# Three fp32r passes for the expert down product, with the first weights split once and streamed from DRAM

## Chip, cores and metric

One core of one Trainium2 chip. The metric is device time of one execution in microseconds. The kernel before has a median of 554.55 us over 3 runs (554.51 to 554.79).

## What is computed

The reference is a stack of four layers over `x` (128 sequences of 32 steps, 128 features). Each layer has a conditioning block and a feed-forward block. The change touches the feed-forward block of layer 0 only. It is a mixture of 8 experts in which each expert chooses `cap = 8` steps of each sequence:

```python
scores = jnp.einsum('BTC,CE->BTE', x, gate_w)
probs = jax.nn.softmax(scores, axis=-1)
top_p, top_idx = jax.lax.top_k(jnp.transpose(probs, (0, 2, 1)), cap)
xin = jnp.take_along_axis(x[:, None, :, :], top_idx[..., None], axis=2)
h = jax.nn.gelu(jnp.einsum('BElC,ECH->BElH', xin, w1), approximate=False)   # C=128, H=512
y = jnp.einsum('BElH,EHC->BElC', h, w2) * top_p[..., None]
out = jnp.zeros((B, T, C), x.dtype).at[b_idx, top_idx].add(y)
```

Before it stands the layer's own mixture of 2 shared and 8 routed experts, which every step passes through. Behind it stand an LSTM, a quantised convolution block, a tanh RNN, a ternary block, a leaky RNN and a gated block, which the change leaves alone apart from three waits at their start.

## The kernel before

Everything is kept transposed (features on the 128 partitions). Every engine's program is written out by hand; semaphores tie them together, and nothing is reordered later. Four stretches matter here.

**Chunk stage.** The steps are cut into 8 chunks of 512 columns. Chunks 0 and 1 are a special start. Each of chunks 2 to 7 (`chunk`) has 12 units, of which every third is a shared one and the rest are routed. For a routed unit TensorE (PE) makes the first product, ScalarE (ACT) the gelu (`routed_gelu`, L452), VectorE (DVE) the multiplication with the gate (`routed_gated`, L456), ACT the high half of the hidden values (`hidden_high`, L372), GpSimd (POOL) the low half (`hidden_low`, L387: values minus high half), and PE the second product. A product of split operands is `product`: three fp32r matmuls (L325 high·high, L326 high·low, L327 low·high). First products run 3 units ahead of second ones. In the unit with index 3, ACT also makes the high half of the next chunk's x, and POOL the low half behind unit 6 (L318).

**Expert stage.** 4 groups of 8 tiles, 8 experts in each, and 2 halves (b = 0, 1) of each expert's 512 hidden rows: 64 steps w. `expert_up(w)` is `product` twice over 256 columns into a PSUM bank; ACT's gelu (L1442) writes SBUF (`hb`, the old `th` and `pb` tiles); `expert_down(w)` is 2 plain fp32 matmuls with `w2` (L1248, two records each in the trace); DVE copies the result out (`output_copy`, L1382). PE issues `expert_up(w + 3)` and then `expert_down(w)`. The first weights of each expert are split anew in each group on DVE (`expert_split`, L1219 high, L1221 low; 32 times) into the two tile pairs `sw1_hl` and `sw3_hl`.

**Beside the experts.** In group g the tokens of group g+1 are gathered: one-hot tables on DVE (L1160), token halves (L1172 ACT, L1180 DVE), gather products on PE (L1198) behind steps 5, 7, 9 and 11, copies out on ACT (L1210). The results of group g are turned (L1299, behind step 14 and behind the next group's first step), copied by ACT (L1308), and scattered (L1316) with tables from DVE (L1371). Group 0 also makes the second half of the choice of steps (softmax with a table load on ACT at L1058, top 8 on DVE at L1081 and L1082, rows to DRAM at L1096) and the mean absolute weights (L219) that POOL's preparation of later weights needs.

**SP's queue.** SyncE (SP) issues all DMAs in order: expert weights with two 256 KB loads a chunk (`load_expert`), the gates' rows, the gather rows (L1155), raw weights (L206), slot rows (L1103), convolution taps (L211).

Of the kernel before, what the change touches and what calls it, by code (L numbers as in the profile page):

```python
# [15 lines left out]
P = 128  # L16
# [3 lines left out]
E = 8  # L20
# [33 lines left out]
def build_program(nc, t, out):  # L54
# [8 lines left out]
    with ctx:  # L63
# [32 lines left out]
        with ExitStack() as layer0:  # L96
# [4 lines left out]
            gate_w = sb0("gate_w", [P, E])  # L101
            w1 = sb0("w1", [P, E, H0])
            w2 = sb0("w2", [P, E, HT, C])

# [16 lines left out]
            i_dram = nc.dram_tensor("topi_scratch", [NTILE, SLOT_TILE], F32, kind="Internal").ap()  # L121

# [3 lines left out]
            s_wmoe, s_gw, s_wffn, s_sw2 = [sem(f"s_wmoe{k}") for k in range(5)], sem("s_gw"), sem("s_wffn"), sem("s_sw2")  # L126
# [87 lines left out]
            def weight_sums():  # L214

                dve.wait_ge(s_w1, n_late)
                dve.wait_ge(s_raw, 48)
                for k, w in enumerate(raw_weights()):
                    dve.tensor_reduce(wsum[:, k:k + 1], w, X, ALU.add, apply_absolute_value=True).then_inc(s_sum, 1)  # L219
# [47 lines left out]
            cst = in_x1("cst", 1024, CHUNK)  # L267
            th = [sb0(f"th{k}", [P, CHUNK]) for k in range(2)]
            pb = [sb0(f"pb{k}", [P, CHUNK]) for k in range(2)]
# [21 lines left out]
            ctok_low0 = sb0("ctok_low0", [P, CHUNK], F32R)  # L291
            stage_b = layer0.enter_context(ExitStack())
# [171 lines left out]
            def chunk(c, par, last=False):  # L464
# [29 lines left out]
                for u, (kind, j) in enumerate(units):  # L494
# [31 lines left out]
                for u, (kind, j) in enumerate(units):  # L526
# [31 lines left out]
                    if c == CHOICE_CHUNK + 1 and u == 4:  # L558
                        choice_rows(0)
                if last:  # L560
                    for q in range(2):
                        gather_copy(q, (1,), dve, s_gxl)
                    dve.wait_ge(s_wffn, 32 * E)
                    expert_split(0)
                    for q in range(2, 4):
                        gather_copy(q, (1,), dve, s_gxl)
                    expert_split(1)
                if not last:
                    load_gate_rows(c + 1, 1 - par)
                if c == 2:  # L570
# [10 lines left out]
                load_expert(c)  # L581

            def load_expert(c):
                sp.dma_start(w1[:, ds(c, 1), :], t["f_w1"][:, ds(c, 1), :]).then_inc(s_wffn, 16)
# [2229 lines left out]
```

## Time and profile before

| what | value |
|---|---|
| runs | 554.51, 554.55, 554.79 us |
| span of the profiled execution, first to last instruction | 553.3 us |
| what lies around it, from the runs' median | 1.25 us |
| PE busy | 540.1 us, 98% |
| DVE, ACT, POOL busy | 425.7, 380.6, 197.8 us |
| chain that ended last | PE 81%, DVE 12%, ACT 4%, issue 2%, POOL 1% |
| granted PE clock | full in all 40 slices |

The page gives the span of the profiled execution; its own time is not shown apart from that. A matmul's recorded duration includes the part that overlaps the next one, so the cost of a matmul in a stream is read from start to start, or from the chain, and not from its mean duration. The same holds for ACT and DVE: an instruction that waits for nothing starts about 0.1 us before the one ahead of it has ended.

### The profile page before, as it was taken

The page shows a single profiled execution, that of the slowest core. Times are in us where ns is not written, and L with a number is a line of the kernel's source. Part 1 is how long each engine was busy: PE and PEld are TensorE (multiplying, and loading weights), DVE is VectorE, ACT ScalarE, POOL GpSimd, SP SyncE. Part 2 cuts the span into 40 slices and gives each one's busy share as a digit, 9 for nine tenths or more (in the row PEclk, how much of TensorE's full clock was granted, in tenths as well). Part 3 has the DMA queues.
Part 4 walks back from the last instruction along what each step waited for, and adds up shares of the span by engine and source line. Part 5 has one row for each costly group of instructions (what it writes and reads, how often), then busy time and mean ns, then how long its engine had stood idle before and what let it go on. Part 6 is the DMA issues. An engine that isn't in the chain of part 4 may idle for free.

```text
span 553.3 us, 10078 instructions
## 1 busy us (share of the span) xinstructions
PE 540.1 (98%) x3341; PEld 468.0 (85%) x3341; DVE 425.7 (77%) x1026; ACT 380.6 (69%) x857; POOL 197.8 (36%) x186
## 2 busy tenths in 40 slices
PE   8999999999999999999999989999999999999997
PEld 7877888887887899999999877788989999987785
DVE  4987656567659779676856359998999999999866
ACT  4567767758767664454552246888988888888965
POOL 4688788788788402947100000010000000000100
PEclk9999999999999999999999999999999999999999
DMA  8634306512081302021000000122111111112211
GB/s 285 194 152 159 152 1 230 191 56 97 2 305 43 124 10 82 1 73 62 2 1 1 0 1 2 20 39 21 21 20 20 21 31 30 34 38 47 45 52 39
DMA packets 30227, 37.36 MB, mean 68 GB/s; under 512 B 20096, under 2 KB 23648, under 8 KB 29280
## 3 DMA queue, kind: packets, MB, share of 16 engines
q1 hardware_dynamic: 30176, 36.72, 21.2%
q8 instruction: 28, 0.46, 0.4%
q14 instruction: 23, 0.19, 0.1%
HBM read 30.24 MB, written 2.28 MB: 59 GB/s over the span
## 4 chain that ended last, share of the span: by engine, by line
PE 81%; DVE 12%; ACT 4%; issue 2%; POOL 1%; DVEq 0%; ACTq 0%
PE bank L325 11%; PE bank L1248 10%; PE bank L327 10%; PE bank L326 10%; PE bank L1673 4%; PE bank L1759 4%; PE bank L1663 4%; PE bank L1700 3%; PE bank L1701 3%; PE bank L1316 2%; PE bank L1198 1%; PE bank L1748 1%; PE bank L1786 1%; PE bank L409 1%; PE bank L1772 1%
## 5 line engine op out<-in xcount | busy, mean ns | idle before, releaser
L387 POOL TENSOR_TENSOR hidden_low<-hidden,hidden_high 128x512 fp32r<-128x512 f32 x72 | 94.4, 1318 | 24.6 <-ACT hidden_high L372 22.4
L2054 POOL CAST h_high<-h 128x256 fp32r<-128x256 f32 x15 | 6.4, 426 | 197.6 <-ACT h L1865 191.2
L452 ACT ACTIVATE bank<-bank 128x512 f32<-128x512 f32 x56 | 32.6, 583 | 34.5 <-PE bank L327 34.3
L456 DVE TENSOR_TENSOR hidden<-bank,big 128x512 f32<-128x512 f32 x56 | 38.5, 688 | 15.8 <-ACT bank L452 14.6
L372 ACT CAST hidden_high<-hidden 128x512 fp32r<-128x512 f32 x70 | 43.0, 615 | 3.3 <-DVE hidden L456 1.9
L1700 PE MATMUL bank<-taps_high,q1T 128*128 128x512 f32 x94 | 42.9, 457 | 1.0 <-ACT q1T L1828 0.6
L325 PE MATMUL bank<-xin_high,sw_high 128*128 128x256 f32 x128 | 43.9, 343 | 0.0
L1701 PE MATMUL bank<-taps_low,q1T 128*128 128x512 f32 x94 | 37.1, 395 | 0.0
L1382 DVE COPY yT<-bank 128x256 f32<-128x256 f32 x32 | 13.6, 424 | 30.4 <-PE bank L1248 30.4
L1801 ACT ACTIVATE gates_t<-bank,lstm_b_half 128x128 f32<-128x128 f32 x96 | 28.2, 364 | 12.2 <-PE bank L1673 8.8
L1663 PE MATMUL bank<-x,lstm_wx 128*128 128x128 f32 x256 | 34.4, 277 | 1.7 <-ACT gates_t L1801 0.9
L326 PE MATMUL bank<-xin_low,sw_high 128*128 128x256 f32 x128 | 36.1, 282 | 0.0
L327 PE MATMUL bank<-xin_high,sw_low 128*128 128x256 f32 x128 | 35.9, 280 | 0.0
L1663 PEld LDWEIGHTS bank<-x,lstm_wx 128*128 128x128 f32 x256 | 32.0, 191 | 4.4 <-ACT gates_t L1801 3.3
L1442 ACT ACTIVATE pb<-bank 128x512 f32<-128x512 f32 x32 | 19.5, 608 | 22.7 <-PE bank L327 22.7
L1673 PE MATMUL bank<-hL,lstm_wh 128*128 128x128 f32 x256 | 34.1, 276 | 0.5 <-DVE hL L1927 0.4
L1673 PEld LDWEIGHTS bank<-hL,lstm_wh 128*128 128x128 f32 x256 | 32.3, 192 | 2.4 <-DVE hL L1927 1.4
L998 POOL TENSOR_TENSOR hidden_low<-hidden,hidden_high 128x512 fp32r<-128x512 f32 x24 | 30.8, 1287 | 9.4 <-ACT hidden_high L778 9.0
L1248 PE MATMUL bank<-pb,w 128*128 128x256 f32 x128 | 32.8, 378 | 0.0
L1248 PE MATMUL bank<-th,w 128*128 128x256 f32 x128 | 32.7, 378 | 0.0
L1759 PE MATMUL bank<-g,ffn_w 128*128 128x256 f32 (+1 forms) x136 | 30.7, 368 | 0.0
L1874 ACT ACTIVATE g<-bank,ffn_b 128x256 f32<-128x256 f32 (+1 forms) x68 | 27.6, 467 | 1.0 <-PE bank L1749 0.6
(270 smaller groups left out, 1736.6 us busy)
## 6 DMA issues: line engine op xcount, KB each, us to landing
big<-gates_scratch SPq DMA_DIRECT2D x7, 2048.0 KB, 8.1
w<-in_f_w SPq DMA_DIRECT2D x16, 256.0 KB, 6.2
onehot<-topi_scratch SPq DMA_DIRECT2D x8, 512.0 KB, 4.2
outT<-x SPq DMA_DIRECT2D x15, 128.0 KB, 2.1
xT<-in_xT SPq DMA_DIRECT2D x3, 512.0 KB, 7.4
hidden<-in_ffn_w SPq DMA_DIRECT2D x3, 256.0 KB, 5.2
hidden<-in_conv_w SPq DMA_DIRECT2D x3, 256.0 KB, 4.8
xT<-in_xT SPq DMA_DIRECT2D x2, 256.0 KB, 4.2
```

The costliest lines, as they stand in the source:

```text
L325: pe.matmul(dst, wh[:, cols], vh[:, :], start=start, stop=False)
L326: pe.matmul(dst, wh[:, cols], vl[:, :], start=False, stop=False)
L327: return pe.matmul(dst, wl[:, cols], vh[:, :], start=False, stop=stop)
L372: act.copy(hidden_hl[u % 3][0][:, :], hidden[u % 3][:, :]).then_inc(s_hi, 1)
L387: pool.tensor_tensor(hidden_hl[u % 3][1][:, :], hidden[u % 3][:, :], hidden_hl[u % 3][0][:, :].bitcast(F32), ALU.subtract).then_inc(s_lo, 1)
L456: dve.tensor_tensor(hidden[u % 3][:, :].rearrange("p (i k) -> p i k", k=P), r_bank[j % 2][:, :].rearrange("p (i k) -> p i k", k=P), gate_r ...
L1248: mm = pe.matmul(y_bank[e % 2][:, 0:SLOT_GE], w2[:, e, ht, :], hb[w % 4][:, i * SLOT_GE:(i + 1) * SLOT_GE], start=(ht == 0), stop=(ht == H ...
L1663: mm = pe.matmul(gate_ps(t, q), lstm_wx[:, q * P:(q + 1) * P], x1[:, t, :], start=(0 < t < EARLY or (t > 0 and q == 0)), stop=(t == 0), sk ...
L1673: mm = pe.matmul(gate_ps(t, q), lstm_wh[:, q * P:(q + 1) * P], hL[:, (t - 1) % 2, :], start=(t == 0), stop=(t > 0), skip_group_check=True)
L1700: pe.matmul(dst, q, taps_high[:, 2 - j, :], start=True, stop=False)
L1701: pe.matmul(dst, q, taps_low[:, 2 - j, :], start=False, stop=True).then_inc(c_taps, 1)
L1759: mm = pe.matmul(bank_down(v), ffn2_w2[:, f, :], part(g2[:, f, :, :], v), start=(f == 0), stop=(f == HT - 1))
```

## The change

The down product becomes `product` with `w2` and the gelu's result both split: 6 fp32r matmuls a step in place of 2 fp32 ones. `w2` is split once, in place. The gelu (`expert_gelu`) now writes back into its PSUM bank, ACT makes the high half of it (`expert_high`), DVE the low half (`expert_low`), in 3 buffer pairs in place of 4 buffers. `w1` is split once in the chunk stage (ACT high, DVE low, at the units in `PARTS_AT`, and `w2` 3 units behind each), its halves are stored to DRAM and loaded for each expert of each group (32 times, 512 KB) into one of 3 tile pairs. `expert_split` goes. Core of the diff:

```diff
+            w2_high = nc.alloc_sbuf_tensor_at("w2_high", [P, E, H0], F32R, offset=at_w1)
+            w2_low = nc.alloc_sbuf_tensor_at("w2_low", [P, E, H0], F32R, offset=at_w2)
+            w1_dram = nc.dram_tensor("w1_parts_scratch", [E, 2, P, H0], F32, kind="Internal").ap()
...
@@ chunk, ACT
+                    if n * c + u in PARTS_AT:
+                        w1_high_part(PARTS_AT.index(n * c + u))
+                    if n * c + u - 3 in PARTS_AT:
+                        w2_high_part(PARTS_AT.index(n * c + u - 3))
@@ chunk, DVE
+                    if n * c + u - 1 in PARTS_AT:
+                        w1_low_part(PARTS_AT.index(n * c + u - 1))
+                    if n * c + u - 4 in PARTS_AT:
+                        w2_low_part(PARTS_AT.index(n * c + u - 4))
                 if last:
-                    for q in range(2):
+                    for q in range(4):
                         gather_copy(q, (1,), dve, s_gxl)
-                    dve.wait_ge(s_wffn, 32 * E)
-                    expert_split(0)
...
+                for e in STORE_PARTS[c]:
+                    store_parts(e)
...
+            PARTS_AT = (28, 35, 42, 49, 55, 73, 79, 85)
+            STORE_PARTS = {2: (0,), 3: (1, 2), 4: (3, 4), 5: (5,), 6: (), 7: (7,)}
...
+            def w1_low_part(e):
+                dve.wait_ge(s_w1hi, e + 1)
+                dve.tensor_tensor(w1_third[1][:, :], w1[:, e, :], w1_third[0][:, :].bitcast(F32), ALU.subtract
+                                  ).then_inc(s_w1lo, 1)
...
+            def load_parts(k):
+                if k == 0:
+                    sp.wait_ge(s_ab, 2 * NSH * NCHUNK)
+                    sp.wait_ge(s_w1st, 32 * E)
+                if k >= 3:
+                    sp.wait_ge(s_h, 2 * (k - 2))
+                for part_no, dst in enumerate(w1_hl[k % 3]):
+                    sp.dma_start(dst[:, :].bitcast(F32), w1_dram[k % E, part_no]).then_inc(s_w1ld[k % 3], 16)
...
@@ expert_up
-                    pe.wait_ge(s_es, 2 * (g * E + e + 1))
+                    pe.wait_ge(s_w1ld[k % 3], 32 * (k // 3 + 1))
...
-                    pe.wait_ge(s_hg, w - 3)
+                    pe.wait_ge(s_hbl, w - 3)
@@ expert_down
-                pe.wait_ge(s_hg, w + 1)
+                pe.wait_ge(s_hbl, w + 1)
...
-                    mm = pe.matmul(y_bank[e % 2][:, 0:SLOT_GE], w2[:, e, ht, :], hb[w % 4][:, i * SLOT_GE:(i + 1) * SLOT_GE],
-                                   start=(ht == 0), stop=(ht == HT - 1))
+                    h_parts = [hl[w % 3][:, i * SLOT_GE:(i + 1) * SLOT_GE] for hl in (hb_high, hb_low)]
+                    mm = product(y_bank[e % 2][:, 0:SLOT_GE], (w2_high[:, e, :], w2_low[:, e, :]),
+                                 slice(ht * P, (ht + 1) * P), h_parts, ht == 0, ht == HT - 1)
...
+            def expert_gelu(w):
+                act.wait_ge(s_h, w + 1)
+                act.activation(h_bank[w % 4][:, :], h_bank[w % 4][:, :], ACT.Gelu).then_inc(s_hg, 1)
+
+            def expert_high(w):
+                act.wait_ge(s_hg, w + 1)
...
+                if w >= 3:
+                    act.wait_ge(s_y2, w - 2)
+                act.copy(hb_high[w % 3][:, :], h_bank[w % 4][:, :]).then_inc(s_hbh, 1)
+
+            def expert_low(w):
+                dve.wait_ge(s_hbh, w + 1)
...
+                dve.tensor_tensor(hb_low[w % 3][:, :], h_bank[w % 4][:, :], hb_high[w % 3][:, :].bitcast(F32), ALU.subtract
+                                  ).then_inc(s_hbl, 1)
...
@@ group_sp
+                for e in range(E):
+                    k = g * E + e + 3
+                    if k < GROUPS * E:
+                        load_parts(k)
+                    if g == 0 and e == 3:
+                        choice_store(1)
+                    if g == 0 and e == 4:
+                        sp.wait_ge(s_vc, 64)
+                        load_slots(1)
```

DVE's order in a group is rewritten around `expert_low`; the four weight sums (`weight_sum`) are spread over two experts; the tap loads move from behind group 2 into groups 1 and 2.

**ACT at the start of the expert stage** (`th`, `pb`, `bank` and `hb` are the gelu's targets, `sel` is the softmax's). Before:

```order
L417 COPY cst<-bank 128x512
L1210 CAST xin_high<-bank 128x8x64
L1442 ACTIVATE th<-bank 128x512 x2
L1058 ACT_TABLE_LOAD
L1058 ACTIVATE sel<-score 128x128
L1442 ACT_TABLE_LOAD
L1442 ACTIVATE pb<-bank 128x512
```

and with the change:

```order
L1315 ACTIVATE bank<-bank 128x512
L1323 CAST hb_high<-bank 128x512
L1315 ACTIVATE bank<-bank 128x512
L1323 CAST hb_high<-bank 128x512
L1121 ACT_TABLE_LOAD
L1121 ACTIVATE sel<-score 128x128
L1315 ACT_TABLE_LOAD
L1315 ACTIVATE bank<-bank 128x512
L1323 CAST hb_third<-bank 128x512
```

Two casts now stand ahead of the two table loads, and one more between them and the third step's down product.

**DVE in group 0, around the second half of the choice.** With the change (L1329 is `expert_low`, L1461 the output copy, L1144 and L1145 the top 8, L1153 the last of the rows, L1226 a one-hot table, L1450 scatter tables):

```order
L1461 COPY yT<-bank 128x8x32
L1329 TENSOR_TENSOR hb_low<-bank,hb_high 128x512
L1246 TENSOR_TENSOR ctok_low<-ctok,ctok_high 128x512
L1144 MAX topv<-probT 128x8
L1145 MAX_INDEX topi<-topv,probT 128x8
L1144 MAX topv<-probT 128x8
L1145 MAX_INDEX topi<-topv,probT 128x8
L1152 CAST topf<-topi 128x32
L1153 TENSOR_TENSOR topf<-topf,seq_off 128x32
L1226 TENSOR_SCALAR onehot<-onehot,part 128x1024
L1450 TENSOR_SCALAR scat<-iota_tok,slot_cols 128x128 x2
L1329 TENSOR_TENSOR hb_low<-bank,hb_high 128x512
```

A low half on which a down product waits now stands behind all of these, where a weight split stood.

**SP in group 0.** With the change (L646 loads the two halves of one expert's weights, L1159 stores the rows of the choice, L1166 loads the slot rows):

```order
L646 DMA w_third_high<-w_parts_scratch 128x512
L646 DMA w_third_low<-w_parts_scratch 128x512
L646 DMA sw_high<-w_parts_scratch 128x512
L646 DMA sw_low<-w_parts_scratch 128x512
L1159 DMA topi_scratch<-topf 128x32
L1159 DMA topv_scratch<-topv 128x32
L646 DMA sw_high<-w_parts_scratch 128x512
L646 DMA sw_low<-w_parts_scratch 128x512
L1166 DMA slot_rows<-topi_scratch 32x128
```

The load for the group's last expert stands behind the store of the rows.

## Rows read from the trace of the kernel before

**Rows 1.** The page: busy time, share of the span and instructions by engine

```profile
PE 540.1 (98%) x3341; PEld 468.0 (85%) x3341; DVE 425.7 (77%) x1026; ACT 380.6 (69%) x857; POOL 197.8 (36%) x186
```

**Rows 2.** Chain that ended last, 284 to 330 us: start us, us, what

```profile
285.25 0.86 PE bank L1248 x4
286.82 0.86 PE bank L1248 x4
```

**Rows 3.** Timeline of PE, down products of steps 0 and 2: start us, us

```profile
192.40 1.03 PE L1248 MATMUL bank<-th,w 128*128 128x256 f32 x4
...
195.99 1.03 PE L1248 MATMUL bank<-pb,w 128*128 128x256 f32 x4
```

**Rows 4.** Timeline of ACT at the start of the expert stage

```profile
190.44 1.32 ACT L1442 ACTIVATE th<-bank 128x512 f32<-128x512 f32 x2 [1.87 <-PE bank L327]
191.78 1.28 ACT L1058 ACT_TABLE_LOAD   x1
...
193.41 1.28 ACT L1442 ACT_TABLE_LOAD   x1
194.70 0.60 ACT L1442 ACTIVATE pb<-bank 128x512 f32<-128x512 f32 x1
```

**Rows 5.** Timeline of DVE in group 0

```profile
205.86 0.18 DVE L1081 MAX8 topv<-probT 128x8 f32<-128x32 f32 x1
...
206.99 0.19 DVE L1090 TENSOR_TENSOR topf<-topf,seq_off 128x32 f32<-128x32 f32 x1
207.22 0.75 DVE L1160 TENSOR_SCALAR onehot<-onehot,part 128x1024 fp32r<-128x1024 f32 x1
207.88 1.11 DVE L1371 TENSOR_SCALAR scat<-iota_tok,slot_cols 128x128 f32<-128x128 f32 x4
```

**Rows 6.** Timeline of SP in group 0: issue of the rows' two stores

```profile
207.21 0.33 SPq L1096 DMA_DIRECT2D topi_scratch<-topf  x1
207.58 0.43 SPq L1096 DMA_DIRECT2D topv_scratch<-topv  x1
```

**Rows 7.** DMA view: loads, KB each, median us from issue to landing

```profile
w<-in_f_w SPq DMA_DIRECT2D x16, 256.0 KB, 6.2
...
big<-in_s_w1T SPq DMA_DIRECT2D x1, 256.0 KB, 3.6
```

**Rows 8.** Timelines of PE and ACT at the end of group 0

```profile
218.18 1.06 PE L1299 MATMUL bank<-ident,yT 128*128 128x128 f32 x8
...
218.90 1.07 ACT L1308 COPY ysl<-bank 128x512 f32<-128x512 f32 x2 [4.08 <-PE bank L1299]
219.86 1.11 ACT L1442 ACTIVATE th<-bank 128x512 f32<-128x512 f32 x2
```

**Rows 9.** Page, groups: busy us, mean ns of one, idle before it and releaser

```profile
L387 POOL TENSOR_TENSOR hidden_low<-hidden,hidden_high 128x512 fp32r<-128x512 f32 x72 | 94.4, 1318 | 24.6 <-ACT hidden_high L372 22.4
...
L452 ACT ACTIVATE bank<-bank 128x512 f32<-128x512 f32 x56 | 32.6, 583 | 34.5 <-PE bank L327 34.3
L456 DVE TENSOR_TENSOR hidden<-bank,big 128x512 f32<-128x512 f32 x56 | 38.5, 688 | 15.8 <-ACT bank L452 14.6
```

**Rows 10.** Timelines of POOL and DVE in chunk 7, and of DVE at 255 us

```profile
178.59 1.82 POOL L387 TENSOR_TENSOR hidden_low<-hidden,hidden_high 128x512 fp32r<-128x512 f32 x1 [0.83 <-ACT hidden_high L372]
...
178.56 0.68 DVE L1180 TENSOR_TENSOR ctok_low<-ctok,ctok_high 128x512 fp32r<-128x512 f32 x1
...
254.98 1.64 DVE L1221 TENSOR_TENSOR sw_low<-w,sw_high 128x512 fp32r<-128x512 f32 x1
```

**Rows 11.** Timelines of POOL and PE at units 0 and 7 of chunk 3

```profile
83.59 1.29 POOL L387 TENSOR_TENSOR hidden_low<-hidden,hidden_high 128x512 fp32r<-128x512 f32 x1 [0.88 <-ACT hidden_high L372]
...
85.61 0.39 PE L325 MATMUL bank<-hidden_high,sw_high 128*128 128x512 f32 x1
...
95.61 2.55 POOL L387 TENSOR_TENSOR hidden_low<-hidden,hidden_high 128x512 fp32r<-128x512 f32 x2
...
96.99 0.48 PE L325 MATMUL bank<-hidden_high,rw_high 128*128 128x512 f32 x1
```

**Rows 12.** Waits, 60 to 188 us: us in total, times, longest us

```profile
PEld bank L325 <- POOL hidden_low L387: 3.4, 12, 0.5
```

More of the change, by code:

```diff
@@ L291, in build_program @@
             ctok_low0 = sb0("ctok_low0", [P, CHUNK], F32R)
+            w1_third = [sb0(f"w1_third_{k}", [P, H0], F32R) for k in ("high", "low")]
+            hb_third = sb0("hb_third", [P, CHUNK], F32R)
             stage_b = layer0.enter_context(ExitStack())
@@ new lines, in build_program, with w2_raw, w1_high_part @@
+            PARTS_AT = (28, 35, 42, 49, 55, 73, 79, 85)
+            STORE_PARTS = {2: (0,), 3: (1, 2), 4: (3, 4), 5: (5,), 6: (), 7: (7,)}
+            s_w1hi, s_w1lo, s_w2hi, s_w2lo, s_w1st = (sem(n) for n in ("s_w1hi", "s_w1lo", "s_w2hi", "s_w2lo", "s_w1st"))
+            s_w1ld = [sem(f"s_w1ld{k}") for k in range(3)]
+            def w2_raw(e):
+                return w2[:, e, :, :].rearrange("p f c -> p (f c)")
+            def w1_high_part(e):
+                act.wait_ge(s_wffn[e], 32)
+                if e:
+                    act.wait_ge(s_w1st, 32 * e)
+                act.copy(w1_third[0][:, :], w1[:, e, :]).then_inc(s_w1hi, 1)
@@ new lines, in store_parts @@
+            def store_parts(e):
+                sp.wait_ge(s_w1lo, e + 1)
+                for k in range(2):
+                    sp.dma_start(w1_dram[e, k], w1_third[k][:, :].bitcast(F32)).then_inc(s_w1st, 16)
+            def load_parts(k):
+                if k == 0:
+                    sp.wait_ge(s_ab, 2 * NSH * NCHUNK)
[4 more added lines that the diff above has]
+                    sp.dma_start(dst[:, :].bitcast(F32), w1_dram[k % E, part_no]).then_inc(s_w1ld[k % 3], 16)
@@ L1137, in build_program @@
             onehot, ctok_hl = [], []
-            w1_hl = (sw1_hl, sw3_hl)
+            w1_hl = (sw1_hl, sw3_hl, w1_third)
+            hb_high = [nc.alloc_sbuf_tensor_at(f"hb{k}_high", [P, CHUNK], F32R, offset=at_th + 4 * CHUNK * k) for k in range(2)] + [hb_third]
+            hb_low = [nc.alloc_sbuf_tensor_at(f"hb{k}_low", [P, CHUNK], F32R, offset=at_pb + 4 * CHUNK * k) for k in range(2)] + [ctok_low0]
             def chosen(g, par):
@@ L1242, in expert_down @@
                 e, b = (w % U2) // 2, w % 2
-                pe.wait_ge(s_hg, w + 1)
+                pe.wait_ge(s_hbl, w + 1)
+                if b == 0 and w < U2:
+                    pe.wait_ge(s_w2lo, e + 1)
                 if b == 0 and w >= 4:
@@ L1266, in build_program @@
             chunk_store_tokens(NCHUNK - 1, 1)
-            hb = th + pb
             stage_b.close()
@@ L1386, in group_sp @@
                 if g == 0:
+                    for k in range(3):
+                        load_parts(k)
                     sp.wait_ge(s_down, NCHUNK * NUNITS)
@@ L1505, in build_program @@
                     prepare_weights()
-                if g == GROUPS - 2:
-                    for k in range(3):
-                        load_tap(k)
             slots_turn_late()
```

126 lines of the change are left out of this document (72 added, 54 removed).

## The prediction

> **What bounds the kernel now.** I read the page's busy times first, then the chain of waits, then the timelines of the expert stage and the chunk stage. PE is busy for 98% of the span, and DVE and ACT for 77% and 69% [rows 1]: a microsecond counts only if PE gets or loses it. In the expert stage the chain runs on PE from one down product to the next. Two of them start 1.57 us apart, and each takes 0.86 us of the chain, so the up product between them takes 0.71 us [rows 2]. ACT, DVE and SP can stay hidden there only as long as what they hand over comes before PE asks for it. In the chunk stage PE also decides, but POOL is near it: a low half takes 1.32 us in the mean, a routed unit takes PE about 1.4 us (6 matmuls of twice the columns of those above, so twice 0.12 us each, less a little), and PE already waits for POOL 12 times, for 3.4 us [rows 9, 12].
>
> **What the change takes away.** An up product is 6 fp32r matmuls of 256 columns, 0.71 us. The new down product is the same 6 matmuls. So a step takes 1.42 us in place of 1.57, and 64 steps give back 64 x 0.15 = **9.6 us**. The 32 weight splits go from DVE, but no time of PE's stands behind them: they ran three experts ahead. In their place come 64 low halves on DVE (0.69 us, by the same kind of instruction with one PSUM operand [rows 9]) and 64 casts on ACT. These are not ahead of anything: gelu, cast, low half, down product are a chain, 0.60 + 0.60 + 0.69 us with some 0.05 us at each hand-over, about 2.0 us. Between an up product and its down product PE issues three others of each kind, 4.3 us, so in an even run the chain is hidden. The terms below are the places where it isn't.
>
> **Start of the stage, +2.1 us.** ACT now does two gelus from 190.44 us and then two table loads with the softmax's exponential, from 191.78 to 194.70, 2.92 us [rows 4]. With the change it does gelu, cast, gelu, cast: 0.60 + 0.04 + 0.50 + 0.60 + 0.04 + 0.59, to 192.81. The loads then end at 195.73, the third gelu at 196.33, its cast at 196.96, its low half at 197.70. PE would ask for it at 195.99 less two shortened down products, 195.69 [rows 3]. The price is 2.1 us; it falls to 0 only if the loads were hidden, which nothing does.
>
> **Steps 3 and 4, +0.5 us.** The token cast stands ahead of gelu 3, and the softmax's sums with the slot copy (about 1.2 us of DVE) ahead of low half 4. By the same adding up they come 0.2 and 0.3 us late. Bounds 0 and 1.
>
> **DVE around the choice, +0.5 us.** Behind the output copy of expert 3 stand low half 9 (0.61 start to start: 0.69 less 0.08, by which the next one starts before its end), the low tokens (0.61), half of the top 8 with the rows (205.86 to 207.22, 1.36), the one-hot table (0.66), two scatter tables (0.52) and low half 10 (0.69) [rows 5]: with the copy's 0.34 and the 0.2 us after which it starts, 5.0 us after down product 7. PE has 5 products and two gathers there (4 matmuls of 0.12 us each), 4.5 us. Bounds 0 and 1.5.
>
> **SP behind the choice, +2.2 us.** The load for expert 7 is behind the rows' stores. The rows are ready 3.1 us after down product 7; the stores take 0.8 us to issue [rows 6], the first half's issue 0.43, and the second half lands 3.6 us after its own issue if nothing is beside it, 6.2 us in company [rows 7]. I take 3.6, since the big loads of that time are over: 7.9 us. PE asks for these weights after two gathers, 6 products and the 0.5 us above, 5.7 us. So 2.2 us late; with 6.2 us, 4.8; with a landing under 1.4 us, 0. The loads of the other experts have 4 up and 5 down products, 6.4 us, from the release of a buffer to its use, against 0.43 + 3.6 = 4.0, and the gathers and transposes lengthen it: nothing.
>
> **Weight sums, +0.1 us.** The fourth one now comes later than PE's sum over them would start, 0.5 us; PE stands for about 0.4 us near there already.
>
> **Group boundaries, +1.5 us.** ACT copies two turned banks before the next group's first gelu: PE's transposes end at 219.24, the gelu starts at 219.86 [rows 8], its cast is done at 221.09, its low half at 221.83. PE wants it 3 products after the transposes, 219.24 + 2.13 = 221.37. So 0.5 us late, three times. Bounds 0 and 3 x 1.
>
> **Chunk stage, +1.5 us.** 16 casts on ACT and 16 subtractions on DVE come in. ACT and DVE idle enough (34.5 us before 56 gelus, 15.8 us before 56 gate products [rows 9]) to take in 0.5 and 0.69 us, not without delay. The point is POOL. When DVE subtracted two SBUF tiles beside POOL's subtraction, POOL's took 1.82 us in place of 1.29; in another place DVE's took 1.64 us in place of 0.69 [rows 10]. So the two don't run side by side, and each split costs POOL 0.5 us. Between the end of a low half and its use PE leaves 0.73 us in most units (84.88 to 85.61) but 0.08 in unit 7 (96.91 to 96.99), behind the next chunk's x [rows 11]. Most splits stand where 0.7 us cover them; of the 16 one stands at unit 7 and three at unit 8, and two in chunk 7, where one-hot tables already hold POOL up. I take 6 x 0.25 us. The bounds are 0 and 16 x 0.5 = 8 us; I am near the low one since the 0.73 us is the usual gap.
>
> The Trainium skill, SBUF — State Buffer, section "SBUF: two separate sides", says that a DVE operation with two SBUF inputs and a GpSimd operation that reads SBUF hold one port pair in turn, for the whole instruction. By that rule each of the 16 would take its full length from POOL; it speaks against this change, and the slower rival goes that way.
>
> **What costs nothing.** The wait for all expert weights at 189 us: they have long landed. The three later waits for the last down product: the output copy behind it was waited for anyway. The moved tap loads: only POOL waits for them, and nothing near waits for POOL. If SP were held up by them, the weights of group 1 or 2 would be late.
>
> **Sum.** -9.6 + 2.1 + 0.5 + 0.5 + 2.2 + 0.1 + 1.5 + 1.5 = -1.2 us. Against the profiled execution the span goes from 553.3 to 552.1; against the median of 554.55 (the span and the 1.25 us around it) to 553.35, **553.3 us** rounded down. This case's own range is 551.5 to 555. About 0.2%, 1.1 us, is what a measurement of this kernel can tell from no change: 553.4 to 555.7.
>
> **Rivals.**
> *Covers hold.* SP's load lands in time, the chunk stage absorbs the splits, and the DVE queue and steps 3 and 4 cost half: -9.6 + 2.1 + 0.5 + 0.1 + 1.5 + 1.0 = -4.4, 550.1 us. For it: the usual 0.73 us, and PE's leads of 3 steps. Against it: the rows' store is in SP's way by the written order.
> *POOL becomes the bound in the chunk stage, slower.* Every split holds POOL or is held by it, the next gate product is late by the 0.95 us that DVE lost, and 0.73 us don't cover both. At 0.45 us a split it costs 7.2 us in place of 1.5: 559.0 us. It decides from 0.17 us a split on (2.8 / 16), where the gain is gone. For it: POOL at 1.32 us against PE's 1.4 can hardly catch up within routed units, and the page's rule stated above. By that rule, the trace agrees in kind; its 0.5 us is less than DVE's whole 0.69.
> *DVE in groups 1 to 3.* The one-hot table and the low tokens ahead of low half 6 leave about 0.05 us by my adding up. With 0.8 us late in each of three groups: 555.7 us.
> *The stream is too slow.* If 512 KB an expert land 1 us late each time, because 16 MB move in 120 us, it is 29 us more: 582. Against it: 4.0 us against 6.4.
>
> **Chances.** Forecast 0.45, covers hold 0.2, POOL 0.2, DVE 0.1, stream 0.05. Range 549.5 to 559.0: it takes in the covers and most of the POOL case, and leaves out the far ends. Faster by over 0.2%: 0.27 of the forecast's share and 0.2, 0.47. Within 0.2%: 0.18 and 0.05, 0.23. Slower: 0.2 + 0.05 + 0.05, 0.30.
>
> **What would show it.** In the chain of the stage, down products 0.71 us and starts 1.42 us apart. A gap of PE before down product 2, released by DVE behind ACT's table loads; one before up product 14, released by a DMA; about 0.5 us at each boundary. In the chunk stage, low halves of 1.8 us on POOL beside the splits, and PE's wait for POOL grown from 3.4 us to about 5. I am wrong if the expert stage shows less than 5 us of PE's idle time, if the chunk stage is longer by over 4 us, or if PE waits for weights in groups 1 to 3.

## The result and the profile after

| | before | after |
|---|---|---|
| median of 4 runs, us | 554.53 (554.42 to 554.79) | 574.95 (573.53 to 579.44) |
| span of the profiled execution, us | 553.3 | 578.1 |
| end of the chunk stage (last scores), us | 189.3 | 211.5 |
| group 0 of the expert stage, to its first turned bank, us | 28.9 | 32.3 |
| groups 1 to 3, to the last turned banks, us | 98.7 | 97.6 |

The change makes the kernel slower by 20.4 us: the ratio is 1.038, with a 95% interval from 1.0335 to 1.042. I had predicted 553.3 and a range up to 559.0, so it is wrong, and by a cost that lies almost whole in the chunk stage, which is 22.2 us longer in the profiled execution. The groups of the expert stage lost 3.4 and won 1.1 us there. These stages add up to 24.5 us and not to 20.4: the profiled execution of after is the slowest of its four (579.44 us, mean granted clock 0.982; the others 573.53 to 575.82 us, 0.988 to 0.994), so its share of lost clock is larger than that of the median.

The page of after, busy times and the clock in 40 slices, against [rows 1]:

```profile
PE 544.5 (94%) x3469; PEld 471.7 (82%) x3469; DVE 450.6 (78%) x1042; ACT 421.1 (73%) x937; POOL 198.6 (34%) x186
...
PEclk9999989698999999999999999999999999999998
...
L397 POOL TENSOR_TENSOR hidden_low<-hidden,hidden_high 128x512 fp32r<-128x512 f32 x72 | 97.3, 1362 | 43.3 <-ACT hidden_high L382 42.0
L466 DVE TENSOR_TENSOR hidden<-bank,big 128x512 f32<-128x512 f32 x56 | 38.3, 686 | 22.7 <-ACT bank L462 21.1
```

PE was busy for 98% of the span and is now for 94%. POOL's low half is hardly longer (1362 against 1318 ns, [rows 9]), but POOL stands 43.3 us before it in place of 24.6, so POOL is not the bound: it is itself kept waiting by ACT, and ACT by something else. The clock row dips three times, which it didn't before (the last digit is the end of the program, where PE is idle). The chain of waits shows the largest single piece, 87 to 105 us:

```profile
87.09 0.43 SPq L603
...
88.52 0.43 SPq L446
88.95 0.04 issue
89.00 0.43 SPq L636
89.42 0.04 issue
89.47 11.36 DMA w_parts_scratch<-w_third_low
...
100.91 0.07 ACT w_third_high L617
...
102.01 0.54 ACT hidden_high L382
102.55 0.07 issue
102.62 1.27 POOL hidden_low L397
103.89 0.04 issue
103.94 0.79 PE bank L335
```

SP issues the loads of experts 4 and 5 (L602, L603, four of 256 KB), then the 2 MB of gate rows (L446), then the store of expert 1's parts (L636). That store lands 11.36 us after its issue (the gate rows issued ahead of it landed at 99.51 us); the median of its kind is 2.0. Its source is the one staging tile, so ACT's cast of expert 2 (L617) waits for it, 6.89 us, and behind that cast in ACT's queue stand the gelu and the high half that POOL and PE need.

All gaps of PE in the chunk stage that weren't there before, in the timeline of PE (in brackets the idle time before the instruction, and who ended it):

```profile
77.56 0.50 PE L335 MATMUL bank<-hidden_high,rw_high 128*128 128x512 f32 x1 [0.96 <-POOL hidden_low L397]
...
103.94 0.79 PE L335 MATMUL bank<-hidden_high,sw_high 128*128 128x512 f32 x1 [5.16 <-POOL hidden_low L397]
...
132.29 0.50 PE L335 MATMUL bank<-hidden_high,rw_high 128*128 128x512 f32 x1 [1.25 <-POOL hidden_low L397]
...
177.37 0.51 PE L335 MATMUL bank<-hidden_high,rw_high 128*128 128x512 f32 x1 [1.27 <-POOL hidden_low L397]
...
193.60 0.50 PE L335 MATMUL bank<-hidden_high,sw_high 128*128 128x512 f32 x1 [1.52 <-POOL hidden_low L397]
...
200.73 0.50 PE L335 MATMUL bank<-hidden_high,sw_high 128*128 128x512 f32 x1 [1.41 <-POOL hidden_low L397]
...
202.61 0.51 PE L335 MATMUL bank<-hidden_high,rw_high 128*128 128x512 f32 x1 [0.21 <-POOL hidden_low L397]
```

And the table of stretches for PE (busy time and count, granted clock, DMA share, GB/s), all stretches of 4 us in which the clock was below 1.00:

```profile
76.00:80.00 4.00, 3.04 (x16) 0.91 0.00 0
80.00:84.00 4.00, 4.00 (x13) 0.66 0.00 0
100.00:104.00 4.00, 0.06 (x1) 0.90 0.01 4
104.00:108.00 4.00, 3.99 (x9) 0.50 0.65 210
108.00:112.00 4.00, 4.00 (x15) 0.50 0.55 189
112.00:116.00 4.00, 4.00 (x16) 0.82 0.51 197
132.00:136.00 4.00, 3.71 (x16) 0.74 0.34 128
136.00:140.00 4.00, 4.00 (x16) 0.83 0.55 197
```

These two views account for the loss. The seven gaps are 11.8 us. A gap costs up to 0.27 us more than its bracket says: the matmul before it is drawn to its modelled end (0.39 us, where the next one starts after 0.23 in an even run), 0.16, and the first one behind it can hold the next up by 0.11 (201.07 less 200.73, against 0.23). That makes 13.7 us at most. The missing clock is 4 us x (0.09 + 0.34 + 0.10 + 0.50 + 0.50 + 0.18 + 0.26 + 0.17) = 8.6 us. Together 22.3, where 22.2 were lost. That it fits to 0.1 is partly luck. Start by start against before, the gaps cost 12.9 us and the low clock about 7.8 (part of the 8.6 fell while PE stood idle anyway), and the other 1.5 are delays of 0.1 to 0.3 us each, too short to be printed as gaps. The granted clock of 0.50 behind the longest gap is the lower of PE's two levels, 1.2 GHz.

What the gaps come from is the question for the experiments. **Theory A:** the store's place in SP's queue, with the clock's fall behind the long gap. **Theory B:** the 16 subtractions of two SBUF tiles on DVE beside POOL's.

### The profile page after: what moved, and what is told of

Same layout as the page of the kernel before. It is cut to its first block, busy times and chain, and to the rows that moved or that the text cites. A ratio compares the mean times of both kernels' runs of the same rounds, so it can differ in the third digit from the quotient of the medians.

```text
span 578.1 us, 10522 instructions
## 1 busy us (share of the span) xinstructions
PE 544.5 (94%) x3469; PEld 471.7 (82%) x3469; DVE 450.6 (78%) x1042; ACT 421.1 (73%) x937; POOL 198.6 (34%) x186
## 4 chain that ended last, share of the span: by engine, by line
PE 60%; DVE 17%; ACT 11%; issue 6%; POOL 4%; DMA 2%; SPq 0%; DVEq 0%; ACTq 0%
PE bank L335 8%; PE bank L336 7%; PE bank L337 7%; PE bank L1767 4%; PE bank L1853 4%; PE bank L1757 4%; PE bank L1794 3%; PE bank L1795 3%; POOL hidden_low L397 2%; DMA w_parts_scratch<-w_third_low 2%; PE bank L1395 2%; ACT bank L1315 2%; DVE hidden L466 2%; PE bank L419 1%; PE bank L1842 1%
## 5 line engine op out<-in xcount | busy, mean ns | idle before, releaser
L397 POOL TENSOR_TENSOR hidden_low<-hidden,hidden_high 128x512 fp32r<-128x512 f32 x72 | 97.3, 1362 | 43.3 <-ACT hidden_high L382 42.0
L462 ACT ACTIVATE bank<-bank 128x512 f32<-128x512 f32 x56 | 32.6, 583 | 30.0 <-PE bank L337 29.4
L382 ACT CAST hidden_high<-hidden 128x512 fp32r<-128x512 f32 x70 | 42.9, 613 | 15.1 <-DVE hidden L458 12.0
L1315 ACT ACTIVATE bank<-bank 128x512 f32<-128x512 f32 x64 | 38.3, 598 | 12.7 <-PE bank L337 12.2
L1329 DVE TENSOR_TENSOR hb_low<-bank,hb_high 128x512 fp32r<-128x512 f32 x43 | 29.4, 684 | 6.6 <-ACT hb_high L1323 6.3
L1767 PEld LDWEIGHTS bank<-hL,lstm_wh 128*128 128x128 f32 x256 | 32.3, 192 | 2.4 <-DVE hL L2021 1.4
L1059 POOL TENSOR_TENSOR hidden_low<-hidden,hidden_high 128x512 fp32r<-128x512 f32 x24 | 30.8, 1288 | 9.5 <-ACT hidden_high L839 8.9
L335 PE MATMUL bank<-hidden_high,rw_high 128*128 128x512 f32 x64 | 27.8, 435 | 3.8 <-POOL hidden_low L397 3.7
L335 PE MATMUL bank<-x_high,rw_high 128*128 128x512 f32 x64 | 28.1, 439 | 0.3 <-DVE hidden L466 0.3
L335 PE MATMUL bank<-xin_high,sw_high 128*128 128x256 f32 x88 | 25.7, 292 | 1.7 <-DMA sw_low<-w_parts_scratch 1.4
L1323 ACT CAST hb_high<-bank 128x512 fp32r<-128x512 f32 x43 | 25.2, 587 | 2.2 <-PE bank L337 1.1
L1461 DVE COPY yT<-bank 128x256 f32<-128x256 f32 x32 | 13.4, 420 | 16.7 <-PE bank L337 16.5
```

The source lines that it names most:

```text
L335: pe.matmul(dst, wh[:, cols], vh[:, :], start=start, stop=False)
L382: act.copy(hidden_hl[u % 3][0][:, :], hidden[u % 3][:, :]).then_inc(s_hi, 1)
L397: pool.tensor_tensor(hidden_hl[u % 3][1][:, :], hidden[u % 3][:, :], hidden_hl[u % 3][0][:, :].bitcast(F32), ALU.subtract).then_inc(s_lo, 1)
L1315: act.activation(h_bank[w % 4][:, :], h_bank[w % 4][:, :], ACT.Gelu).then_inc(s_hg, 1)
L1767: mm = pe.matmul(gate_ps(t, q), lstm_wh[:, q * P:(q + 1) * P], hL[:, (t - 1) % 2, :], start=(t == 0), stop=(t > 0), skip_group_check=True)
```

## Experiments on the chunk stage

**Expert 1's store first (e1_store_first).**

```diff
+                if c == 3:
+                    store_parts(1)
+                    load_expert(4)
+                    load_expert(5)
                 if not last:
                     load_gate_rows(c + 1, 1 - par)
...
-                if c in (2, 3):
-                    load_expert(2 * c)
-                    load_expert(2 * c + 1)
+                if c == 3:
+                    load_expert(6)
+                    load_expert(7)
...
-            STORE_PARTS = {2: (0,), 3: (1, 2), 4: (3, 4), 5: (5,), 6: (), 7: (7,)}
+            STORE_PARTS = {2: (0,), 3: (2,), 4: (3, 4), 5: (5,), 6: (), 7: (7,)}
```

> The changed kernel with another order on SP's queue alone: in chunk 3 the store of expert 1's split up weights goes ahead of the 2 MB load of gate rows and ahead of the loads of experts 4 and 5, which move from the end of chunk 2 to behind it. Theory A (most of the 20.4 us comes from ACT's 6.9 us wait for that store, and from the lower granted clock behind it): ACT's w_third_high of expert 2 waits under 1 us, the clock of the stretch 84 to 125 us returns to above 0.95, and the time falls by 8 to 13 us, to 562 to 567. Theory B (most comes from VectorE's 16 subtractions of two SBUF tiles beside GpSimd's): the wait goes but the time falls by 4 us at most, to 571 or more.

Measured: 567.42 us (ratio to before 1.023, 1.022 to 1.025), 7.5 less. ACT's wait is gone, PE is busy for 20.74 of the 21 us from 84 on (15.84 before this edit), and the chunk stage ends at 199.3. It falls just short of A's 8 us, and A is not the whole: 10.0 us of the chunk stage's growth stay. The clock is 1.00 from 84 to 125 but falls once, later (0.73 and 0.84 from 164 to 172), behind a gap of 1.28 us; that is 1.7 us.

**No subtractions of weights (e2_no_w_subtract).** This kernel leaves out the low parts of the expert weights.

```diff
-                dve.tensor_tensor(w1_third[1][:, :], w1[:, e, :], w1_third[0][:, :].bitcast(F32), ALU.subtract
+                dve.tensor_tensor(w1_third[1][:, 0:8], w1[:, e, 0:8], w1_third[0][:, 0:8].bitcast(F32), ALU.subtract
...
-                dve.tensor_tensor(w2_low[:, e, :], w2_raw(e), w2_high[:, e, :].bitcast(F32), ALU.subtract
+                dve.memset(w2_low[:, e, :].bitcast(F32), 0.0
```

> The changed kernel without the arithmetic of the 16 subtractions of weights in the chunk stage: the low part of w1 is 8 columns and its store reads the high tile instead, the low part of w2 is set to zero by a memset on VectorE at the same place; casts on ACT, stores, streams, waits and the expert stage stay. The low parts of the expert weights are left out of the result. Theory B (port): GpSimd's hidden_low falls back from 1362 ns to near 1318, PE's waits for it in the chunk stage from 19 us to under 7, and the time falls by 8 to 13 us, to 562 to 567. Theory A (store wait and clock): ACT's wait of 6.9 us stays, and the time falls by 3 us at most.

Measured: 569.61 us (1.026, 1.023 to 1.028), 5.3 less. ACT's wait is there (6.5 us), and the clock is at 0.50 from 100 to 108 behind PE's gap of 4.77 us. Neither theory's number holds: A gave 3 us at most, B at least 8. What B said of POOL came true in part: the mean of its low half fell from 1362 to 1309 ns, but PE's waits for it (those of its weight loads) only from 19.0 to 11.1 us, where B gave under 7. The subtraction of 8 columns says why B was still underrated by this edit. DVE's timeline, and POOL's at the same time:

```profile
179.00 1.25 DVE L621 TENSOR_TENSOR w_third_low<-w,w_third_high 128x8 fp32r<-128x8 f32 x1
180.18 0.68 DVE L453 SCALAR_TENSOR_TENSOR pb<-th,bank 128x512 f32<-128x512 f32 x1
...
178.70 1.53 POOL L397 TENSOR_TENSOR hidden_low<-hidden,hidden_high 128x512 fp32r<-128x512 f32 x1 [0.17 <-ACT hidden_high L382]
```

A subtraction of 8 columns takes 1.25 us, and ends at 180.25, when POOL's instruction ends (180.23). The median of the eight is 1.20 us, and each of them, from 0.53 to 1.25 us long, ends within 0.03 us of the end of a POOL instruction. So DVE doesn't share with POOL: it waits for POOL's whole instruction to end, and its queue stands. The edit took the work away but kept this wait for half of the 16.

**Both (e3_both).** The two diffs together.

> Both edits together: the store of expert 1 first, and no subtractions of weights. If A and B are the whole of the growth of the chunk stage, the expert stage starts within 2 us of where it did before the change (189.6), and the time is 554.5 + 2.4 (what the expert stage lost) = 557, at most 559. If ACT's 16 casts cost the chunk stage something by themselves, it starts later than 192 us and the time is 560 or more.

Measured: 559.84 us (1.010, 1.008 to 1.012), 15.1 less. By the medians the edits gave 7.5 and 5.3 alone, and together 2.3 more than their sum. By the profiled spans (578.1, 566.1, 568.1 and 558.2 us) they gave 12.0 and 10.0 alone and 2.1 less than their sum together; the difference is the clock, of which the profiled execution of after had lost most. In this run the clock no longer falls: PE shows 1.00 in every stretch of 4 us from 60 to 340. The stage ends at 190.9, 1.6 later than before, as expected if A and B are the whole; the time is 0.8 us above the 559 that I gave for that. A and B are thus nearly all of the chunk stage's growth, and beside casts and stores the arithmetic of the subtractions is worth 567.42 less 559.84, 7.6 us.

**The subtractions alone (e4_subtract_alone).** In the kernel before:

```diff
+                    if n * c + u - 1 in PARTS_AT:
+                        extra_subtract(0, 2 * PARTS_AT.index(n * c + u - 1))
+                    if n * c + u - 4 in PARTS_AT:
+                        extra_subtract(1, 2 * PARTS_AT.index(n * c + u - 4) + 1)
...
+                dve.tensor_tensor(extra[k][:, :], xT[:, 0:CHUNK], xT[:, CHUNK:2 * CHUNK], ALU.subtract).then_inc(s_extra, 1)
```

> The kernel before, with nothing of the change, plus 16 VectorE subtractions of two SBUF tiles of 128x512 into a spare tile, at the 16 places where the change has those of the weights. Nobody waits for them. Theory B: the 16 cost 0.5 to 0.8 us each on the path, and the time is 554.5 + 8 to 12 = 562 to 567. Theory A: they are hidden, and the time is 554.5 to 557. My term of the prediction for this was +1.5 (556.0).

Measured: 559.15 us (1.008, 1.006 to 1.010), 4.5 more than before, between what the theories gave. By itself a subtraction costs 0.28 us of the end, where my forecast had 0.09. All 16 together, with POOL's group:

```profile
L593 DVE TENSOR_TENSOR extra<-xT x16: 684/1356/1785, 68.8 to 176.9; 128x512 f32<-128x512 f32 x16
```

```profile
L388 POOL TENSOR_TENSOR hidden_low<-hidden,hidden_high 128x512 fp32r<-128x512 f32 x72 | 98.4, 1379 | 24.0 <-ACT hidden_high L373 21.6 <-DVE hidden_high L383 1.4
```

The median is 1356 ns in place of some 690, and POOL's mean rises from 1318 to 1379 ns: 72 x 0.061 = 4.4 us that POOL takes longer over the same work: it waits for DVE too, as the rows below show.

**The casts alone (e7_casts_alone).** The same with `act.copy(extra[k][:, :], xT[:, 0:CHUNK])` at the 16 places on ACT.

> The kernel before plus 16 casts of 128x512 on ACT alone, at the 16 places where the change casts the weights; nobody waits for them. With both the subtractions and the store wait gone the chunk stage was still 1.6 us later than before. If that is the casts, the time is 554.7 + 1 to 2, 555.7 to 556.7; if ACT's idle time takes them in, it stays within 0.5 us of 554.7.

Measured: 554.66 us against 554.75 (1.000, 0.999 to 1.001). The casts alone cost nothing. Casts and subtractions together cost more than both alone. With the store's wait gone the chunk stage is 10.0 us longer (e1). Of that, 1.6 stay without the arithmetic (e3, which keeps casts, stores and semaphores), 3.6 are what the subtractions cost alone (192.9), 1.7 are clock, and 3.1 or more are left (e3 keeps some of the waits of the subtractions, so 1.6 and 3.6 overlap). One gap of PE in e1, 1.26 us at 120 us, can be followed back to a place where the two meet. ACT, DVE and POOL there:

```profile
110.26 0.62 ACT L630 CAST w_high<-w 128x512 fp32r<-128x512 f32 x1
110.78 0.58 ACT L462 ACTIVATE bank<-bank 128x512 f32<-128x512 f32 x1
...
111.46 0.69 DVE L466 TENSOR_TENSOR hidden<-bank,big 128x512 f32<-128x512 f32 x1 [1.16 <-ACT bank L462]
112.06 1.75 DVE L634 TENSOR_TENSOR w_low<-w,w_high 128x512 fp32r<-128x512 f32 x1
113.73 0.68 DVE L453 SCALAR_TENSOR_TENSOR pb<-th,bank 128x512 f32<-128x512 f32 x1
...
111.97 1.29 POOL L397 TENSOR_TENSOR hidden_low<-hidden,hidden_high 128x512 fp32r<-128x512 f32 x1 [0.24 <-ACT hidden_high L382]
```

and the same place in e4, where no cast stands ahead of the gelu:

```profile
111.00 0.69 DVE L457 TENSOR_TENSOR hidden<-bank,big 128x512 f32<-128x512 f32 x1 [0.64 <-ACT bank L453]
111.61 0.73 DVE L593 TENSOR_TENSOR extra<-xT 128x512 f32<-128x512 f32 x1
112.26 0.68 DVE L444 SCALAR_TENSOR_TENSOR pb<-th,bank 128x512 f32<-128x512 f32 x1
...
111.73 1.76 POOL L388 TENSOR_TENSOR hidden_low<-hidden,hidden_high 128x512 fp32r<-128x512 f32 x1
```

PE is at the same point in both to 0.3 us. In e4 the subtraction starts 0.12 us ahead of POOL's instruction: it takes 0.73 us, and POOL's takes 1.76 in place of 1.29. In e1 ACT's cast makes the gelu, and with it the product and the subtraction, 0.46 us late. Now POOL's instruction is 0.09 us ahead, and the subtraction takes 1.75 us. The products behind it in DVE's queue come 1.47 us later than in e4, and from there the chain leads over POOL's x_low and a low half of 1.71 us, which waits for the next subtraction, to PE at 120.14. So the cast costs nothing by itself, but it decides who waits for whom. I had priced the two in one term as if slack could be used twice. A run with casts and subtractions alone, without the stores, wasn't made.

## Experiments on the expert stage

PE's gaps in the expert stage of after are, in group 0, 1.70 us behind the table loads, 0.62 before a one-hot gather, 1.36 for expert 7's weights and 0.46 for the weight sums; in groups 1 to 3 eight of 0.37 to 1.04 us, 4.7 in all. With 0.26 us of filling for each they are 5.2 and 6.8 us, against a gain of 2.4 and 7.2 from shorter down products (which do start 0.71 us behind the up product's start, as predicted).

**Three moves (e5_stage_order)** on the kernel with expert 1's store first:

```diff
-                    if g == 0 and e == 3:
+                    if g == 0 and e == 4:
                         choice_store(1)
...
-                    if g < GROUPS - 1 and u in (2, 6):
+                    if g < GROUPS - 1 and u in ((0, 4) if g else (2, 6)):
                         tokens_high(act, g + 1, u // 4)
...
                     expert_high(w)
+                    if g and u == 0:
+                        if g == 1:
+                            act.wait_ge(s_sum, MEANS)
+                        slots_out(g - 1, 0)
```

with `tokens_low` moved in the same way on DVE, and `slots_out(g, 0)` taken from the end of the group.

> The kernel of the run that stores expert 1 first (567.4), with three moves in the expert stage: in group 0 the loads of expert 7's parts go ahead of the choice's stores on SP; in groups 1 and 2 tokens_high and tokens_low come one step earlier; ACT copies the turned banks of a group behind the first gelu and cast of the next one. Theory C (the gain of the down product is lost at single places where PE waits for what stands ahead on ACT, DVE and SP): PE's gaps for the DMA (1.36 us), for the one-hot tables in groups 1 and 2 (0.50 and 1.04) and at the boundaries (0.49, 0.41, 0.42) go, each with some 0.2 us of filling PE again, and the time falls by 3 to 5 us, to 562.4 to 564.4. Theory D (ACT and DVE are near full, and a wait taken away comes back elsewhere): it falls by under 1.5 us.

Measured: 564.29 us (1.017, 1.015 to 1.019), 3.1 less. Each theory holds for a part. Groups 1 to 3 went from 98.1 to 95.3 us, although the clock fell there in this run and not in e1 (0.66 and 0.91 from 264 to 272, 1.7 us): the boundaries and the one-hot gaps are gone (C). Group 0 stayed at 32.3 us: expert 7's weights are on time, but in place of their 1.29 us in e1 PE waits 0.67 us for a low half on DVE and 1.16 in place of 0.54 for the weight sums (D). DVE was the next bound right behind the DMA.

**No table loads (e6_no_table_loads)**, on top:

```diff
-                               tiles_of(score, h).rearrange("p i e -> p (i e)"), ACT.Exp).then_inc(s_ac, 1)
+                               tiles_of(score, h).rearrange("p i e -> p (i e)"), ACT.Tanh, scale=0.5).then_inc(s_ac, 1)
...
+                dve_c(dve.tensor_scalar(tiles_of(score, h), ex, -1.0, 1.0, ALU.mult, ALU.add))
+                dve_c(dve.reciprocal(tiles_of(score, h), tiles_of(score, h)))
+                dve_c(dve.scalar_tensor_tensor(ex, ex, 1.0, tiles_of(score, h), ALU.add, ALU.mult))
```

> The run before this one, and the choice's exponential computed as (1 + tanh(x/2)) / (1 - tanh(x/2)) from the table that ACT already holds: no table loads, three small DVE instructions more. By the chain the two loads cost 1.7 us and the filling of PE in group 0: the time falls by a further 1.7 to 2.2 us against it. If ACT's queue was late for another reason, it falls by under 1 us.

Measured: 566.31 us (1.020, 1.018 to 1.022), 2.0 more, a miss. In group 0 the gap of 1.7 us became one of 0.45, and the group 31.1 us in place of 32.3. But the choice of the first half of the tokens lies in chunk 5. Its three added instructions hold DVE's queue from 134.65 to 136.91 us, ahead of a gate product; PE has two gaps of 0.77 and 1.03 us there, and the clock went to 0.58 from 140 to 144 us. The profiled chunk stage ends at 205.3 in place of 199.6. Not all of that is the edit: the clock also fell from 76 to 84 and from 168 to 176 us, behind gaps of 0.94 and 1.26 us. The run before has gaps of 0.92 and 1.28 us at these two places, and its clock stayed at 1.00 there. By the stretches of 4 us the clock makes up 3.4 of the 5.7 us.

**The splits in group 0 (v0, v1, v2).** The runs so far say where the change should not work: in the chunk stage. In the kernel before, DVE splits w1 in the expert stage anyway. So this version leaves the chunk stage and group 0's fp32 down products as they were, stores DVE's splits from there, casts w2 on ACT and subtracts it on POOL (idle from 187 to 218 us), and takes three passes in groups 1 to 3 alone. The gain to be had is 48 x 0.15 = 7.2 us.

```diff
+            def store_parts(e):
+                sp.wait_ge(s_es, 2 * (e + 1))
+                for part_no, src in enumerate(w1_hl[e % 3]):
+                    sp.dma_start(w1_dram[e, part_no], src[:, :].bitcast(F32)).then_inc(s_w1st[e], 16)
...
+            def w2_low_part(e):
+                pool.wait_ge(s_w2hi, e + 1)
+                pool.wait_ge(s_y2, 2 * (e + 1))
+                pool.tensor_tensor(w2_low[:, e, :], w2_raw(e), w2_high[:, e, :].bitcast(F32), ALU.subtract
...
+                    if w >= U2:
+                        h_parts = [hl[(w + 2) % 3][:, i * SLOT_GE:(i + 1) * SLOT_GE] for hl in (hb_high, hb_low)]
+                        mm = product(y_bank[e % 2][:, 0:SLOT_GE], (w2_high[:, e, :], w2_low[:, e, :]),
+                                     slice(ht * P, (ht + 1) * P), h_parts, ht == 0, ht == HT - 1)
+                        continue
                     mm = pe.matmul(y_bank[e % 2][:, 0:SLOT_GE], w2[:, e, ht, :], hb[w % 4][:, i * SLOT_GE:(i + 1) * SLOT_GE],
```

> The kernel before, with its chunk stage and its group 0 (down products on fp32 weights) unchanged. In group 0, DVE's splits of w1 are stored to DRAM, ACT casts w2's high part and GpSimd subtracts its low part behind each expert's last down product; groups 1 to 3 stream w1 back and take the down product in three passes, as the change does. Theory (the loss is in the chunk stage and group 0, the down product gives 0.15 us each): groups 1 to 3 gain the 1.0 us that they gained in the change, the first 190 us are as before, group 0 is at most 1 us longer: 553 to 554.5. If GpSimd beside DVE's splits holds group 0 up (8 subtractions of 1.3 us), 556 or more.

Measured: 561.33 us (1.011, 1.009 to 1.013), a miss by 7 us. PE stood 1.21 us for a split of DVE that had waited for POOL (its cast, with one SBUF operand, took 1.49 us beside POOL's subtraction in place of 0.42), and 3.48 us for the first weights of group 1: their load stood on SP behind the last store and the choice's stores. The clock fell behind that (0.62 from 220 to 224). Groups 1 to 3 show gaps of the same kinds as in the change, and take 99.0 us.

> The run before this one with two of the moves of the expert stage: tokens one step earlier in groups 1 and 2, ACT's copies of the turned banks behind the first gelu and cast of the next group. Theory C: 2.5 to 4 us less than it, 549.5 to 551.5. Theory D: within 1 us of it.

Measured: 556.18 us (1.004, 1.002 to 1.005), 5.2 less than v0, more than the 2.5 to 4 that C gave; the difference holds v0's 1.7 us of clock too. Groups 1 to 3 now take 93.9 us against 98.7 before. The 3.28 us for the weights and the 1.22 us for the split stand in group 0.

v2 moves what these point to:

```diff
+                    for e in range(3, E - 1):
+                        store_parts(e)
+                    load_parts(E)
+                    store_parts(E - 1)
+                    choice_store(1)
...
-                pool.wait_ge(s_y2, 2 * (e + 1))
+                pool.wait_ge(s_y2, 2 * (e + 3))
...
+                    if g == 1 and e == 6:
+                        slots_copy(1, m_bank[0])
                     if tables_at <= e < tables_at + 4:
```

> The run v1 (556.2) with what PE still waited for taken away: on SP in group 0 the first stores go ahead of the one-hot loads, and the load of group 1's first weights ahead of the last store and the choice's stores (PE waited 3.28 us for that load); GpSimd's subtractions of w2 come two experts later, so that they meet fewer of DVE's splits (1.22 us); in group 1 the slot columns are copied ahead of two scatter tables (0.95 us); the taps move to group 3 (1.09 us before a one-hot table). Theory C: each gap goes, with 0.2 us of filling, and the time is 556.2 less 5 to 7, 549 to 551: faster than before. Theory D: waits come back elsewhere, and it is above 553.

Measured: 551.06 us (549.57 to 552.46) against 554.75: ratio 0.994, 0.992 to 0.996. This is faster than the kernel before by 3.7 us and than the change by 24, at the upper edge of C's 549 to 551. The profiled execution is the fastest of its six (549.57 us). The table of stretches, group 0 and groups 1 to 3 (times as their bounds, then busy PE), of v2:

```profile
188.60:217.50 28.90, 28.90 (x193) 1.00 0.78 257
217.50:311.30 93.80, 91.66 (x772) 1.00 0.47 149
```

and of before:

```profile
189.30:218.20 28.90, 28.90 (x193) 1.00 0.28 94
218.20:316.90 98.70, 98.09 (x676) 1.00 0.07 20
```

Group 0 takes the same 28.9 us although it now holds the stores, the casts of w2 and its subtractions on POOL, and groups 1 to 3 give 4.9 of the 7.2 us. What is left there is one gap of 1.20 us before a down product in group 2, released by DVE's low half, one of 0.33, and smaller ones.

## Why the prediction was wrong

The step that failed is "Chunk stage, +1.5 us", with bounds of 0 and 8. It measured 22.2 us in the profiled execution, and it failed in three ways.

1. **A missing wait.** I costed POOL and DVE, and in "What costs nothing" the waits for the loads; the wait of ACT for the store of the expert before, through one staging tile and behind 3 MB on SP's queue, is in no term. With what it did to the clock it is 7.5 us by the medians and 12.0 by the profiled executions (e1). I followed SP's queue to those who wait for it only in the expert stage.
2. **The port, mis-sized.** I read the slower POOL and DVE instructions of [rows 10] as a loss of 0.5 us in 0.73 us of slack, and took 6 x 0.25. The subtractions alone measured 4.5 us (e4), and 7.6 beside the casts (e1 against e3). DVE waits for the end of POOL's instruction, what stands behind it in DVE's queue waits too, and POOL's next instruction then waits for DVE. I had priced POOL's 0.5 us alone, and [rows 10] show both sides. The rival "POOL becomes the bound" had the sign and the place, at 7.2 us; that price was near for the subtractions, but the engine that became late was not POOL alone. The rule of the Trainium skill that the prediction cites (SBUF — State Buffer, section "SBUF: two separate sides"), a lock held for the whole instruction, had it right. The trace agrees: a subtraction of 8 columns takes up to 1.25 us and ends with POOL's instruction.
3. **Costs that don't add.** Casts alone 0, subtractions alone 4.5; both with stores on time, 567.4 less 554.5 is 12.9, of which the expert stage has 2.8. And the clock: I had no term for it, since before shows 1.00 everywhere. It cost 8.6 us in the profiled run.

In the expert stage the terms can be compared one by one.

- *Down product, -9.6*: right. Up and down products take 0.71 us each.
- *Table loads, +2.1*: a gap of 1.70 and its filling, 2.0. Right. (197.70 less 195.69 in the working is 2.0, not 2.1.)
- *Steps 3 and 4, +0.5*: no gap of PE is printed there.
- *SP behind the choice, +2.2*: 1.36 and filling, 1.6. Right in kind; but with it taken away nothing was won (e5), since low half and weight sums on DVE were late behind it. As a term of a sum it was worth 0.
- *DVE around the choice, +0.5*: a gap of 0.62 before the gather, 0.9 with filling. *Weight sums, +0.1*: 0.46.
- *Group 0* comes to +3.4; my terms for it sum to -2.4 + 5.4 = +3.0. That the sum is so near is in part luck: a term of 0.5 isn't there, one of 0.1 is 0.46, one of 2.2 is 1.6.
- *Boundaries, 3 x 0.5*: gaps of 0.49, 0.41 and 0.42, so 0.7 each with filling.
- *Groups 1 to 3*: -7.2 + 1.5 = -5.7 forecast, -1.1 measured. What was missing are the gaps of DVE's one-hot tables (0.50 and 1.04; the rival "DVE in groups 1 to 3" had them, at 2.4 us), one of 0.63 for ACT's copy of gathered tokens, one of 0.37 before the first product of group 3 (by the code it waits for such a copy too), one of 0.85 before a turned bank, and the filling of 0.26 us at every gap, in no term of mine. In v2 the turned bank came on time, with the slot columns copied ahead of two scatter tables.

Of what I said would show me wrong, "the chunk stage is longer by over 4 us" came true: PE's wait for POOL, which was to grow from 3.4 us to about 5, grew to 19.0. PE never waited for weights in groups 1 to 3.

Open: how e1's 10.0 us divide between single casts and single subtractions. I followed one of its gaps only; whether what is left over is all of the kind seen there isn't shown.

## What to carry to other kernels

When work is moved into a stage where PE is fed by a chain over ACT, DVE and POOL, list for each engine's queue everything that the new instruction may wait for, the store of its own staging tile included, and who stands behind it; a store behind megabytes of loads on the same queue lands when they do. The prices of two insertions measured one by one don't give the price of both, since one can change the order in which the other meets its neighbour. Put such work where the engines' queues have no deadline soon: in the chunk stage the splits and their stores cost 22 us, and 10 with the store's wait taken away. In group 0, where w1 was split anyway and POOL was free to subtract w2, they cost nothing once the queues were in order.

## What the hardware showed that I had not expected

- A DVE subtraction with two SBUF operands waits for the end of POOL's running instruction, whatever its size: 128x8 in 1.20 us in the median of eight, 128x512 in 1.7 (both kinds of split in after) against 0.68 where POOL stood idle. It holds the other way as well: a low half on POOL that starts behind such a subtraction takes 1.76 us in place of 1.29. A cast of 128x512 with one SBUF operand took 1.49 us in place of 0.42 beside POOL in v0. A memset of 128x512 at the same places took 485 ns each of eight times.
- PE's clock fell behind gaps of PE, never without one: to 0.50 for 10.2 us behind 5.16 us and again behind 4.77 us (the missing parts of the stretches in the table, doubled). Gaps of about 1 us were hit or miss, and a hit cost 1.7 us: in after it fell behind 0.96 us at 78 us and behind 1.25 us at 132, and behind 1.27 us at 177 it stayed; in e1 it stayed behind 0.95 us at 77. Behind 3.28 us in v1 it stayed too, behind 3.48 us in v0 it fell to 0.62. So a gap's price is uncertain by as much as itself or more. Whether a fall of the clock explains the whole spread isn't shown, but the changed kernel's runs spread far wider (573.5 to 579.4) than those of before, and their mean granted clocks go along with that: 0.982 in the slowest, 0.988 in the next, 0.994 in the two fastest.
